# An eight-stage transformer megakernel on one core: first attention with 16-bit integer exponentials and column-grouped value matmuls, fourth with scores computed twice and weights loaded during the norm

## The chip, the cores and the metric

One Trainium2 chip, one of its cores. The metric is the device time of one execution in microseconds (us). The engines are TensorE (PE, with its weight loads shown apart as PEld), VectorE (DVE), ScalarE (ACT), GpSimd (POOL), SyncE (SP) and the DMA queues.

## The reference, cut to what matters

The activations `x` are 8 batches of 128 tokens of width 256. Four layers follow one another, each a cross attention and a feed-forward block, all residual:

```
x = x + L0_xattn(layernorm(x), ctx)      x = x + L0_ffn(layernorm(x))
x = x + L1_xattn(layernorm(x), ctx)      x = x + L1_ffn(layernorm(x))
x = x + L2_xattn(layernorm(x), ctx)      x = x + L2_ffn(layernorm(x))
x = x + L3_xattn(layernorm(x), ctx)      x = x + L3_ffn(layernorm(x))
```

The change touches two of the eight stages. In L0_xattn, 16 heads of 16 columns attend over all 1024 context tokens, and q, k, v and the probabilities are fake-quantized:

```
def _fq_sym(x, axis):      # scale = max|x| / 127, round, clip
def _fq_unsigned(x, axis): # scale = max(x) / 255, round, clip to 0..255
```

So the largest exponential of a row is 255 steps and every probability is a whole number of steps. In L3_xattn, 16 query heads share 4 key and value heads (4 groups of 4 heads, 16 columns each); each batch attends to its own 128 context tokens, with a linear position bias and a mask:

```
Q = (query @ Wq) / 4;  K = key @ Wk;  V = value @ Wv
scores = Q K^T + slope[head] * (k_pos - q_pos)
scores = where(mask, scores, lowest)
out = softmax(scores) @ V;  return out @ Wo
```

## The kernel before, in words

`program` runs a table of stages, `l0x`, `l0f`, `l1x`, `l1f`, `l2x`, `l2f`, `l3x`, `l3f`. Each is a `norm` block (layer norm and transpose to `x_normT`) and then the block or blocks of the stage itself; within a block each engine has its own instruction list, held together by semaphores. A stage may give `norm` a `Preload`, whose DMAs are issued on SP during the norm.

**First attention (`attention_l0`).** A first block (tiles `l0p_`) makes the quantized operands: `qT` and `kT` with 48 rows, `v` in bf16. The second block (tiles `l0m_`) is a software pipeline over N = 128 steps, one step for one batch b and head h, written out. Per step n:

- PE `score(n)` (L1747): two bf16 matmuls of 512 columns into one of three PSUM tiles `s_ps[n % 3]`; it waits until the exponential of step n-3 has left that tile.
- DVE `top(n)` (L1814): maximum over 1024 columns.
- POOL (L1737): the bias, log 255 minus scale times maximum.
- ACT `exps(n)` (L1794): exponential of 1024 columns to `pf` (f32), with the row sum.
- DVE `rounding(n-2)` (L1820): adds and subtracts a large constant, writing whole numbers in bf16 to `pi`, 4 buffers.
- SP: one DMA transpose `pi` to `pT`, 4 buffers.
- PE `value(n-5)` (L1757): eight matmuls, each with a 128x128 tile of `pT` as weights and 16 columns of `v` moving; the result has tokens on the partitions.

DVE's order in a step is top(n), then rounding(n-2). After a batch of 16 steps come `scale` on DVE (L1824, L1827), `turn_output` on PE (L1766), `keep_output` on ACT (L1800), `output` on PE (L1772) and `add` on DVE (L1832), at fixed steps:

```
SCALE, TURN, KEEP, OUT, ADD = H + LAG, H + LAG + 1, H + LAG + 1, H + LAG + 2, H + LAG + 3
```

with H = 16 and LAG = 5.

**Second attention (`attention_l1`)**, untouched: it computes each score tile twice, once to take the maximum (L824) and once transposed with the maximum folded in as an extra row (L844), so that ACT can write the transposed probabilities straight away. It works on 32-row and 32-column tiles of the array (L824, L844: 32 rows; L860: 32 columns, four column tiles in turn).

**Fourth attention (`attention_l3`).** SP loads four weights and the mask at the start of its own block (L981, L982). POOL makes 16 slope tiles (L991). PE computes V for all batches (L998). Then each batch has a projection of q and k (L1007) and four groups g of four heads; per group: PE `score` (L1013, 512 columns), DVE adds the slope (L1128), applies the mask limit (L1130) and takes the maximum (L1133), ACT makes four exponentials of 128 columns with sums (L1087), PE transposes them (L1019), DVE copies them to SBUF (L1138), PE multiplies with V (L1028). Per batch follow scaling (L1142, L1145), two transposes (L1036), a copy (L1093), the output projection (L1042) and the add (L1151). `carried` (L706) runs the batches in a loop of two.

Of the kernel before, what the change touches and what calls it, by code (L numbers as in the profile page):

```python
# [8 lines left out]
I16 = mybir.dt.int16  # L9
# [929 lines left out]
def attention_l3(pg):  # L939

    nc, G, J, C = pg.nc, 4, 4, 16
    FMAX = float(np.finfo(np.float32).max)
    names = ("w_in", "mask_in", "mask_step", "limits", "rel", "slopes", "proj", "proj_kept", "v_done", "v_kept", "scores", "biased", "steps", "maxed",
             "exped", "p_turned", "p_kept", "pv", "scaled", "o_turned", "o_kept", "out", "added", "recips")
    s = {m: pg.sem(f"l3x_{m}") for m in names}
    with ExitStack() as st:
# [17 lines left out]
        p = sb("p", [P, G, J, P])
        pT = sb("pT", [P, 2, J, P])
        mx = sb("mx", [P, 2, J])
        sm = sb("sm", [P, 2, G, J])
        rs = sb("rs", [P, 2, G, J])
        on = sb("on", [P, 2, D])
        oT = sb("oT", [P, 2, KD, P])  # L970
        pr = [psum(f"pr{i}", [P, G, P]) for i in range(2)]
        s_ps = [psum(f"s{i}", [P, J, P]) for i in range(2)]
        t_ps = [psum(f"t{i}", [P, J, P]) for i in range(2)]
        o_ps = psum("o", [P, 512])
        f_ps = psum("f", [P, 512])
        block = st.enter_context(nc.Block())

        @block.sync
        def _(sp):
            for m, t in (("l3_wq", wq), ("l3_wk", wk), ("l3_wv", wv), ("l3_wo", wo)):  # L980
                sp.dma_start(t[:], pg.dram[m]).then_inc(s["w_in"], 16)  # L981
            sp.dma_start(mask[:], pg.dram["mask"].rearrange("b t -> (b t)").unsqueeze(0).to_broadcast([P, T])).then_inc(s["mask_in"], 16)  # L982

        @block.gpsimd
        def _(pool):
            nc.gpsimd.iota(rel[:], [[1, P]], 0, -1, allow_small_or_imprecise_dtypes=True).then_inc(s["rel"], 1)
            nc.gpsimd.memset(kT[:], 0.0).then_inc(s["rel"], 1)
# [1291 lines left out]
```

## Time and profile before

| | |
|---|---|
| device time, 3 runs | 2201.01, 2208.95, 2210.03 us (median 2208.95) |
| profiled execution | 2183.78 us, span 2181.7 us |
| mean granted TensorE clock | 0.838 |
| busy share PE / DVE / ACT / POOL | 78% / 58% / 40% / 35% |
| instructions | 27158 |
| block `l0m_` of the first attention | 86.5 to 352.3 us |
| block of the fourth attention | 1748.4 to 1922.5 us |

The busy time is a sum over eight stages with different limits, so the two blocks are read by themselves: the span's start is zero, and a stretch is named by its two times. A granted clock of 1.00 is TensorE at 2.4 GHz, 0.50 at 1.2 GHz.

### The profile page before, as it was taken

To read this page: it belongs to the slowest core of one execution; us is meant where nothing else is said; L and a number is where in the kernel's file an instruction comes from. 1 tells how busy PE (TensorE), PEld (TensorE's weight loads), DVE (VectorE), ACT (ScalarE), POOL (GpSimd) and SP (SyncE) were. 2 spreads that over 40 slices of the span, in tenths; PEclk is the share of its full clock that TensorE was granted. 3 is DMA by queue.
4 is the path that set the end of the run, shared out by engine and by line. 5 is a ranking of instruction groups with operands and counts; after the bars stand their busy time and mean duration, and the time that the engine had idled before them with its cause. 6 is when DMAs were issued, how large, how long until landed. Compare 5 with 4: busy or idle time off the path is not lost. (4 is left out here: it accounts for less than half of the span.)

```text
span 2181.7 us, 27158 instructions
## 1 busy us (share of the span) xinstructions
PE 1693.7 (78%) x8684; PEld 1067.4 (49%) x8684; DVE 1259.9 (58%) x2770; ACT 870.7 (40%) x2109; POOL 761.6 (35%) x1440
## 2 busy tenths in 40 slices
PE   6677775999687499994488888888599878845773
PEld 5322223565454255553266666666355566634551
DVE  4889885222654633326688888888522336674335
ACT  2766663111322111113377777777311135421221
POOL 0133231000100298301588888887000020005773
PEclk8755555999787699997799999999799978867897
DMA  1266563111402022111100000000111000044655
GB/s 65 47 138 126 128 134 79 41 36 36 155 1 99 33 68 102 55 52 44 34 1 1 1 1 1 1 1 1 32 36 36 22 28 0 0 173 135 222 182 223
DMA packets 174473, 140.37 MB, mean 64 GB/s; under 512 B 142049, under 2 KB 154849, under 8 KB 170642
## 3 DMA queue, kind: packets, MB, share of 16 engines
q1 hardware_dynamic: 165026, 113.84, 18.2%
q0 software_dynamic: 7104, 23.60, 3.3%
q10 hardware_dynamic: 2224, 1.47, 0.2%
q8 instruction: 59, 0.97, 0.2%
q14 instruction: 60, 0.49, 0.1%
HBM read 85.82 MB, written 19.50 MB: 48 GB/s over the span
## 5 line engine op out<-in xcount | busy, mean ns | idle before, releaser
L1794 ACT ACTIVATE l0m_pf<-l0m_s,l0m_bias,l0x_sq 128x1024 f32<-128x1024 f32 x128 | 154.2, 1204 | 86.9 <-POOL l0m_bias L1737 86.7
L1814 DVE TENSOR_REDUCE l0m_mx<-l0m_s 128x1 f32<-128x1024 f32 x128 | 155.4, 1216 | 35.3 <-PE l0m_s L1747 35.2
L1368 PE MATMUL l2x_pr<-l_w,l2x_xq 128*128 128x512 bf16 x576 | 142.1, 384 | 40.5 <-ACT credits L42 40.5
L1737 POOL TENSOR_SCALAR l0m_bias<-l0m_mx,l0x_nsq 128x1 f32<-128x1 f32 x128 | 79.1, 618 | 261.3 <-DVE l0m_mx L1814 261.3
L318 PE MATMUL l1e_gu<-x_normT,l1e_w 128*128 128x512 f32 x384 | 169.5, 594 | 0.3 <-DVE l1e_h L361 0.3
L1497 DVE TENSOR_SCALAR l2x_raw<-l2x_raw,l2x_mv,l2x_rs 128x128 f32<-128x128 f32 x384 | 128.8, 396 | 21.5 <-POOL l2x_rs L1347 21.1
L1747 PE MATMUL l0m_s<-l0x_kT,l0x_qT 48*128 48x512 bf16 x256 | 131.6, 618 | 12.0 <-PEq L1572 4.1
L359 DVE TENSOR_TENSOR l1e_h<-l1e_sil,l1e_gu 128x512 f32<-128x512 f32 x48 | 33.0, 687 | 165.4 <-ACT l1e_sil L344 157.8
L318 PE MATMUL l0e_gu<-x_normT,l0e_w 128*128 128x512 f32 x272 | 120.1, 595 | 0.0
L318 PEld LDWEIGHTS l1e_gu<-x_normT,l1e_w 128*128 128x128 f32 x384 | 73.3, 191 | 83.4 <-issue 81.0
L1757 PEld LDWEIGHTS l0m_o<-l0x_v,l0m_pT 128*128 128x128 bf16 x1024 | 37.4, 106 | 156.5 <-DMA l0m_pT<-l0m_pi 113.8
L318 PE MATMUL l2e_gu<-x_normT,l2e_w 128*128 128x512 f32 x256 | 113.7, 598 | 0.0
L344 ACT ACTIVATE l1e_sil<-l1e_gu 128x512 f32<-128x512 f32 x48 | 28.7, 597 | 211.0 <-PE l1e_gu L318 211.0
L1347 POOL TENSOR_TENSOR l2x_rs<-l2x_rs,l2x_half 128x4 f32<-128x4 f32 x96 | 107.0, 1115 | 7.5
L1487 DVE BATCH_NORM_STATS2 l2x_bn<-l2x_raw 128x6 f32<-128x128 f32 x384 | 83.2, 278 | 40.7 <-ACT l2x_raw L1436 40.7
L1368 PEld LDWEIGHTS l2x_pr<-l_w,l2x_xq 128*128 128x128 bf16 x576 | 56.9, 99 | 96.5 <-ACT credits L42 40.9
L359 DVE TENSOR_TENSOR l0e_h<-l0e_sil,l0e_gu 128x512 f32<-128x512 f32 x34 | 23.4, 687 | 125.2 <-ACT l0e_sil L344 125.2
L1441 ACT ACTIVATE x_norm<-l2x_s,l2x_mx 128x128 f32<-128x128 f32 x256 | 90.2, 371 | 2.1 <-DVE l2x_mx L1492 2.1
L359 DVE TENSOR_TENSOR l2e_h<-l2e_sil,l2e_gu 128x512 f32<-128x512 f32 x32 | 22.0, 687 | 118.4 <-ACT l2e_sil L344 118.4
L1820 DVE TENSOR_SCALAR l0m_pi<-l0m_pf 128x1024 bf16<-128x1024 f32 x128 | 87.1, 681 | 1.5 <-ACT l0m_pf L1794 1.5
L326 PE MATMUL l1e_y<-l1e_w,l1e_h 128*128 128x256 f32 x384 | 86.6, 379 | 0.0
L1757 PE MATMUL l0m_o<-l0x_v,l0m_pT 128*128 128x16 bf16 x1024 | 48.8, 177 | 48.1 <-DMA l0m_pT<-l0m_pi 36.3
(507 smaller groups left out, 4076.8 us busy)
## 6 DMA issues: line engine op xcount, KB each, us to landing
l3m_w<-in_l_moe SPq DMA_DIRECT2D x16, 1280.0 KB, 6.7
l1e_w<-in_l_ffn SPq DMA_DIRECT2D x24, 384.0 KB, 3.0
l_rows<-zero_row SPq DMA_DIRECT2D x8, 1024.0 KB, 11.1
l_w<-l_rows SPq DMA_DIRECT2D x8, 1024.0 KB, 11.8
l0e_w<-in_l_ffn SPq DMA_DIRECT2D x17, 384.0 KB, 3.0
l2e_w<-in_l_ffn SPq DMA_DIRECT2D x16, 384.0 KB, 3.0
l1e_route<-l_route SPq DMA_DIRECT2D x8, 512.0 KB
l2q_wps<-in_l_wp SPq DMA_DIRECT2D x16, 256.0 KB, 2.7
```

What stands on the lines that cost most here:

```text
L318: last = nc.tensor.matmul(gu[half][:, m, :], w[:, slot, (2 * k + m) * P:(2 * k + m + 1) * P], pg.xnT[:, k, half * HALF:(half + 1) * HALF], ...
L326: last = nc.tensor.matmul(y[:, t, :], h[:, slot, t * P:(t + 1) * P], w[:, slot, WG:CHUNK], start=False, stop=False, skip_group_check=True)
L1347: g.tensor_tensor(rs[:, buf, 1, :], var, half[:, 0], ALU.pow).then_inc(s["rstd"], 1)
L1368: last = nc.tensor.matmul(flat(pr[t % 2][:]), src[:, k, tokens], pg.l2_w3[:, part, k, at:at + W], start=(k == 0 and part == 0), stop=(k == ...
L1441: last = nc.scalar.activation(p[:, a % 2, j, :], s_ps[a % 2][:, j, :], ACT.Exp, bias=mx[:, a % 2, j:j + 1], accum_out=sm[:, a % 2, j:j + 1])
L1487: last = nc.vector.bn_stats(bn[:, (2 * pi[1] + t) % 4, j, :], raw[:, (2 * pi[1] + t) % 4, j, :])
L1497: last = nc.vector.tensor_scalar(raw[:, buf, j, :], raw[:, buf, j, :], mv[:, buf, j, 0:1], rs[:, buf, 1, j:j + 1], ALU.subtract, ALU.mult)
L1747: last = nc.tensor.matmul(s_ps[n % 3][:, g * HALF:(g + 1) * HALF], qT[:, h, b * P:(b + 1) * P], kT[:, h, g * HALF:(g + 1) * HALF], start=T ...
L1757: last = nc.tensor.matmul(o_ps[:, h * C:(h + 1) * C], pT[:, n % 4, k, :], v[:, k, h * C:(h + 1) * C], start=(k == 0), stop=(k == B - 1))
L1794: nc.scalar.activation(pf[:, n % 4, :], s_ps[n % 3][:], ACT.Exp, scale=sq[:, b, h:h + 1], bias=bias[:, n % 4:n % 4 + 1], accum_out=sm[:, b ...
L1814: nc.vector.tensor_reduce(mx[:, n % 4:n % 4 + 1], s_ps[n % 3][:], AX, ALU.max).then_inc(s["maxed"], 1)
L1820: nc.vector.tensor_scalar(pi[:, n % 4, :], pf[:, n % 4, :], ROUND, ROUND, ALU.add, ALU.subtract).then_inc(s["rounded"], 1)
```

## The change

In the first attention: `pf` becomes int16, so the exponential is rounded as ACT writes it, and the rounding becomes a cast from int16 to bf16. `pi` and `pT` have 8 buffers. `v` is laid out with 32 columns per head, the upper 16 zero (a POOL memset in the first block), and is now the weight operand, `pT` the moving one with 128 columns; four heads write to four groups of 32 PSUM partitions. The result has tokens on the columns, so ACT copies it to SBUF (`read_output`), PE turns it back with four transposes (`turn_back`), and DVE scales from there. The steps after a batch lie further apart.

In the fourth attention: weights are a `Preload` during the norm. Projections of all batches run first, 512 columns at a time, and DVE writes `qT` and `kT` with extra rows that carry position, mask and maximum. Scores are computed twice as in the second attention, on 32-row tiles, through a ring of two PSUM tiles; maxima go through a transpose (`turn_max`) and one add (`augment`). V carries a column of ones, so the sums come out of the value matmul. POOL has one iota and 18 memsets. The mask comes over ACT's queue. The batches are written out.

```diff
-            pf = sb("pf", [P, 4, T])
-            pi = sb("pi", [P, 4, T], BF16)
-            pT = sb("pT", [P, 4, B, P], BF16)
+            pf = sb("pf", [P, 4, T], I16)
+            pi = sb("pi", [P, 8, T], BF16)
+            pT = sb("pT", [P, 8, B, P], BF16)
-            SCALE, TURN, KEEP, OUT, ADD = H + LAG, H + LAG + 1, H + LAG + 1, H + LAG + 2, H + LAG + 3
-            STEPS = N + LAG + 4
+            READ, BACK, SCALE, TURN, KEEP, OUT, ADD = (H + LAG + i for i in (0, 3, 4, 7, 7, 10, 11))
+            STEPS = N + LAG + 12
...
+        N, GROUP, LAG = B * H, 4, 6
...
+                def value(m):
+                    b, g = divmod(m, H // GROUP)
+                    for j in range(GROUP):
+                        n = GROUP * m + j
+                        pe.wait_ge(moved[n % 8], 16 * (n // 8) + 16)
+                    if g == 0 and b >= 1:
+                        pe.wait_ge(s["o_read"], b)
                     for k in range(B):
+                        for j in range(GROUP):
+                            last = nc.tensor.matmul(o_ps[32 * j:32 * j + 32, g * P:(g + 1) * P], v[:, k, GROUP * g + j, :],
+                                                    pT[:, (GROUP * m + j) % 8, k, :], start=(k == 0), stop=(k == B - 1))
                     last.then_inc(s["pv"], 1)
+                def turn_back(b):
+                    pe.wait_ge(s["o_read"], b + 1)
+                    if b >= 1:
+                        pe.wait_ge(s["added"], b)
+                    for g in range(H // GROUP):
+                        last = nc.tensor.transpose(f_ps[:, g * P:(g + 1) * P], oS[:, b % 2, g * P:(g + 1) * P], pg.ident[:])
+                    last.then_inc(s["o_back"], 1)
...
+                def read_output(b):
+                    act.wait_ge(s["pv"], (b + 1) * H // GROUP)
+                    nc.scalar.activation(oS[:, b % 2, :], o_ps[:], ACT.Copy).then_inc(s["o_read"], 1)
...
-                    nc.vector.tensor_scalar(pi[:, n % 4, :], pf[:, n % 4, :], ROUND, ROUND, ALU.add, ALU.subtract).then_inc(s["rounded"], 1)
+                    nc.vector.tensor_copy(pi[:, n % 8, :], pf[:, n % 4, :]).then_inc(s["rounded"], 1)
```

```diff
+def l3_preload(pg, stack):
+    return Preload(pg, stack, "l3w", [("wv", [P, KD, 64], d["l3_wv"]), ("wq", [P, KD, 4 * P], d["l3_wq"]), ("wk", [P, KD, P], d["l3_wk"]),
+                                      ("wo", [P, KD, D], d["l3_wo"])])
...
+        ring = [psum(f"r{i}", [P, 2, J * P]) for i in range(2)]
...
+            for i in range(B + 3):
+                if i < B:
+                    score(i, 0)
+                if 0 <= i - 1 < B:
+                    turn_max(i - 1)
+                if i < B:
+                    score(i, 1)
+                if 0 <= i - 2 < B:
+                    value(i - 2)
+                if 0 <= i - 3 < B:
+                    turn_output(i - 3)
+                if 0 <= i - 1 < B:
+                    shift(i - 1, 0)
+                    shift(i - 1, 1)
+                if 0 <= i - 2 < B:
+                    turn_back(i - 2)
+                if 0 <= i - 3 < B:
+                    output(i - 3)
```

Two places on PE show how the order moves. The first is the end of a batch in the first attention; `l0m_s` are scores, `l0m_o` values, `l0m_f` the output path. Before:

```order
L1747 MATMUL l0m_s<-l0x_kT,l0x_qT 128x512 x2
L1757 MATMUL l0m_o<-l0x_v,l0m_pT 128x16 x8
L1766 MATMUL l0m_f<-ident,l0m_on 128x128 x2
L1747 MATMUL l0m_s<-l0x_kT,l0x_qT 128x512 x2
L1757 MATMUL l0m_o<-l0x_v,l0m_pT 128x16 x8
L1772 MATMUL l0m_f<-l0w_wo,l0m_oT 128x256 x2
L1747 MATMUL l0m_s<-l0x_kT,l0x_qT 128x512 x2
```

and with the change:

```order
L1819 MATMUL l0m_s<-l0x_kT,l0x_qT 128x512 x8
L1832 MATMUL l0m_o<-l0m_pT,l0x_v 32x128 x32
L1841 MATMUL l0m_f<-ident,l0m_oS 128x128 x4
L1819 MATMUL l0m_s<-l0x_kT,l0x_qT 128x512 x8
L1832 MATMUL l0m_o<-l0m_pT,l0x_v 32x128 x32
L1847 MATMUL l0m_f<-ident,l0m_on 128x128 x2
L1819 MATMUL l0m_s<-l0x_kT,l0x_qT 128x512 x6
L1853 MATMUL l0m_f<-l0w_wo,l0m_oT 128x256 x2
L1819 MATMUL l0m_s<-l0x_kT,l0x_qT 128x512 x2
```

The value matmuls of four steps stand together after the fourth score, four transposes are new, and the output projection stands three steps behind its transposes instead of one.

The second place is one batch of the fourth attention (`l3x_r` is the ring, `l3x_po` the values). With the change:

```order
L1050 MATMUL l3x_r<-l3x_kT,l3x_qT 128x128 x8
L1058 MATMUL l3x_nmT<-ident,l3x_nm 128x128 x4
L1050 MATMUL l3x_r<-l3x_kT,l3x_qT 128x128 x8
L1074 MATMUL l3x_po<-l3x_pT,l3x_v 32x512 x4
L1090 MATMUL l3x_f<-ident,l3x_on 128x128 x2
L1066 MATMUL l3x_r<-l3x_qa,l3x_kT 128x512 x4
L1082 MATMUL l3x_bk<-ident,l3x_oS 128x128 x4
L1096 MATMUL l3x_f<-l3w_wo,l3x_oT 128x256 x2
```

Before, the last quarter of a batch's work in the loop read:

```order
L1013 MATMUL l3x_s<-l3x_kT,l3x_qT 128x512
L1019 MATMUL l3x_t<-ident,l3x_p 128x128 x4
L1036 MATMUL l3x_f<-ident,l3x_on 128x128 x2
L1023 REGISTER_ALU
L1028 ISA
L1028 MATMUL l3x_o<-l3x_v,l3x_pT 128x16 x4
L1042 MATMUL l3x_f<-l3x_wo,l3x_oT 128x256 x2
```

The score, transposes and values that came four times per batch are replaced by one longer list per batch, and the projections (16 matmuls per batch before) now stand ahead of the first score.

## Rows read from the trace of the kernel before

**Rows 1.** Busy time by stretch; the columns stand in the first line.

```profile
core 0: us, PE busy (x) PEld busy (x) DVE busy (x) ACT busy (x) POOL busy (x), PEclk, DMA share, GB/s
86.50:352.30 265.80, 194.53 (x1328) 65.18 (x1328) 230.46 (x280) 170.71 (x273) 79.05 (x128) 0.50 0.62 127
99.00:122.00 23.00, 18.63 (x132) 5.41 (x130) 23.00 (x27) 17.31 (x27) 8.31 (x13) 0.50 0.71 151
615.70:621.50 5.80, 5.80 (x66) 3.66 (x58) 2.69 (x3) 1.94 (x2) 0.00 (x0) 0.84 0.01 3
1748.40:1922.50 174.10, 143.18 (x784) 113.40 (x784) 94.41 (x159) 79.47 (x307) 12.88 (x18) 0.81 0.03 9
```

**Rows 2.** Groups by line, 86.5 to 352.3 us: busy, mean ns | idle before, releaser.

```profile
L1814 DVE TENSOR_REDUCE l0m_mx<-l0m_s 128x1 f32<-128x1024 f32 x128 | 155.4, 1216 | 35.3 <-PE l0m_s L1747 35.2
...
L1820 DVE TENSOR_SCALAR l0m_pi<-l0m_pf 128x1024 bf16<-128x1024 f32 x128 | 87.1, 681 | 1.5 <-ACT l0m_pf L1794 1.5
```

**Rows 3.** Timeline of one ordinary step, first attention: start us, us, instruction.

```profile
103.22 0.68 DVE L1820 TENSOR_SCALAR l0m_pi<-l0m_pf 128x1024 bf16<-128x1024 f32 x1
...
103.24 0.38 PE L1757 MATMUL l0m_o<-l0x_v,l0m_pT 128*128 128x16 bf16 x8 [0.26 <-DMA l0m_pT<-l0m_pi]
103.40 0.64 POOL L1737 TENSOR_SCALAR l0m_bias<-l0m_mx,l0x_nsq 128x1 f32<-128x1 f32 x1 [1.09 <-DVE l0m_mx L1814]
...
103.69 1.03 PE L1747 MATMUL l0m_s<-l0x_kT,l0x_qT 48*128 48x512 bf16 x2
103.82 1.21 DVE L1814 TENSOR_REDUCE l0m_mx<-l0m_s 128x1 f32<-128x1024 f32 x1
104.07 1.21 ACT L1794 ACTIVATE l0m_pf<-l0m_s,l0m_bias,l0x_sq 128x1024 f32<-128x1024 f32 x1 [0.44 <-POOL l0m_bias L1737]
...
104.96 0.68 DVE L1820 TENSOR_SCALAR l0m_pi<-l0m_pf 128x1024 bf16<-128x1024 f32 x1
```

**Rows 4.** Timeline behind the first batch of the first attention.

```profile
129.08 2.08 PE L1772 MATMUL l0m_f<-l0w_wo,l0m_oT 128*128 128x256 f32 x4 [1.91 <-ACT l0m_oT L1800]
...
131.09 1.03 PE L1747 MATMUL l0m_s<-l0x_kT,l0x_qT 48*128 48x512 bf16 x2
...
132.06 0.38 PE L1757 MATMUL l0m_o<-l0x_v,l0m_pT 128*128 128x16 bf16 x8
132.16 1.22 DVE L1814 TENSOR_REDUCE l0m_mx<-l0m_s 128x1 f32<-128x1024 f32 x1 [3.38 <-PE l0m_s L1747]
...
132.37 1.03 PE L1747 MATMUL l0m_s<-l0x_kT,l0x_qT 48*128 48x512 bf16 x2
...
133.48 0.27 POOL L1737 TENSOR_SCALAR l0m_bias<-l0m_mx,l0x_nsq 128x1 f32<-128x1 f32 x1 [4.57 <-DVE l0m_mx L1814]
```

**Rows 5.** Groups by line and shape: DVE, 1024 elements of two bytes.

```profile
L1172 DVE TENSOR_SCALAR l2q_step<-l2q_z 128x1024 int16<-128x1024 int16 x8 | 4.0, 500 | 0.3
...
L1173 DVE TENSOR_SCALAR l2q_step<-l2q_step 128x1024 bf16<-128x1024 bf16 x8 | 3.4, 427 | 0.3
```

**Rows 6.** Timeline of the second attention: values (L860), scores (L824), shifted scores (L844).

```profile
620.14 0.61 PE L860 MATMUL l1x_po<-l1x_pT,l1x_ones 128*32 128x256 f32 x8
...
620.57 0.61 PE L860 MATMUL l1x_po<-l1x_pT,l1x_vz 128*32 128x256 f32 x8
...
621.55 1.16 PE L844 MATMUL l1x_r<-l1x_qa,l1x_cb 32*128 32x256 f32 x16
...
623.84 0.73 PEld L824 LDWEIGHTS l1x_r<-l1x_cb,l1x_qm 32*128 32x128 f32 x8 [0.17 <-ACT l1x_pT L890]
...
628.08 1.15 PE L860 MATMUL l1x_po<-l1x_pT,l1x_vz 128*32 128x256 f32 x8
...
628.93 1.15 PE L860 MATMUL l1x_po<-l1x_pT,l1x_ones 128*32 128x256 f32 x8
```

**Rows 7.** Groups by line, page: f32 matmuls of 512 columns in a dense stage.

```profile
L318 PE MATMUL l1e_gu<-x_normT,l1e_w 128*128 128x512 f32 x384 | 169.5, 594 | 0.3 <-DVE l1e_h L361 0.3
```

**Rows 8.** Timeline of the fourth attention: its V matmuls, then its last batches.

```profile
1754.22 7.09 PE L998 MATMUL l3x_s<-l3x_wv,ctxT 128*128 128x64 f32 x32 [6.53 <-DMA l3x_wo<-in_l_wo]
...
1912.96 0.44 PE L1036 MATMUL l3x_f<-ident,l3x_on 128*128 128x128 f32 x2 [0.82 <-DVE l3x_on L1145]
...
1914.05 1.11 PE L1042 MATMUL l3x_f<-l3x_wo,l3x_oT 128*128 128x256 f32 x4
...
1914.99 0.60 PE L1019 MATMUL l3x_t<-ident,l3x_p 128*128 128x128 f32 x4
...
1922.10 0.42 DVE L1151 TENSOR_TENSOR x_res<-x_res,l3x_f 128x256 f32<-128x256 f32 x1 [2.38 <-PE l3x_f L1042]
```

**Rows 9.** Groups by line, 1748.4 to 1922.5 us: DVE waiting for scores.

```profile
L1128 DVE TENSOR_TENSOR l3x_sc<-l3x_s,l3x_slope 128x512 f32<-128x512 f32 x32 | 22.0, 687 | 50.5 <-PE l3x_s L1013 50.4
```

More of the change, by code:

```diff
@@ new lines, in attention_l3 @@
+        nmT, po, bk, f = (psum(m, [P, J * P]) for m in ("nmT", "po", "bk", "f"))
+        banks = [ring[0][:, 0], ring[0][:, 1], ring[1][:, 0], ring[1][:, 1], nmT[:], po[:], bk[:], f[:]]
+        block = st.enter_context(nc.Block())
+        jobs = [("q", 0, j) for j in range(J)] + [("k", 0, 0), ("k", 1, 0)] + [("q", 1, j) for j in range(J)]
+        kept_after = []
+        for what, half, j in jobs:
+            kept_after.append((kept_after[-1] if kept_after else 0) + (4 if what == "k" else 1))
@@ L1032, in turn_output @@
-            def turn_output(b, u):
-                pe.wait_ge(s["scaled"], b + 2)
-                pe.wait_ge(s["added"], b + 1)
+            for n, (what, half, j) in enumerate(jobs):
+                if n == 7:
+                    pe.wait_ge(s["v_kept"], 1)
+                elif n >= 8:
+                    pe.wait_ge(s["proj_kept"], kept_after[n - 8])
+                w, src = (wq[:, :, tile(j)], pg.xnT) if what == "q" else (wk[:], pg.ctxT)
+                for k in range(KD):
+                    last = nc.tensor.matmul(banks[n % 8], w[:, k, :], src[:, k, half * HALF:(half + 1) * HALF], start=(k == 0), stop=(k == KD - 1))
+                last.then_inc(s["proj"], 1)
@@ new lines, in score, with turn_max @@
+            def score(b, pr):
+                ps = freed(pe, "s", b, pr)
+                if b == 0 and pr == 0:
+                    pe.wait_ge(s["proj_kept"], kept_after[-1])
+                for j in range(J):
+                    for jj in range(2):
+                        g = 2 * pr + jj
+                        last = nc.tensor.matmul(ps[:, jj, tile(j)], qT[rows(g), j, tile(b)], kT[rows(g), tile(b)], start=True, stop=True)
+                last.then_inc(s["scores"], 1)
+            def turn_max(b):
+                pe.wait_ge(s["maxed"], 2 * b + 2)
+                if b >= 1:
+                    pe.wait_ge(s["augmented"], b)
+                for j in range(J):
+                    last = nc.tensor.transpose(nmT[:, tile(j)], nm[:, b % 2, j, :], pg.ident[:])
+                last.then_inc(s["nm_turned"], 1)
```

383 lines of the change are left out of this document (195 added, 188 removed).

## The prediction

> **What bounds the kernel now.** I read the stretches first. The two blocks that change are 265.8 and 174.1 us of the profiled 2183.78 [rows 1]; nothing else is touched, so the whole answer lies in these two.
>
> In the first attention DVE is busy for 23.00 of 23.00 us in an ordinary stretch, and the granted clock is 0.50 (1.2 GHz) throughout [rows 1]. The timeline says why a step takes what it takes: from one rounding to the maximum behind it 0.60 us, from there to the next rounding 1.14 us, together 1.74 us [rows 3]. Durations overlap a little, so the start-to-start times count, not 1.21 + 0.68. ACT waits 0.44 us in each step for POOL's bias [rows 3], so it isn't the bound. But 128 x 1.74 = 222.7 us is 43.1 us less than the block takes. Most of the rest stands behind each batch: PE waits 1.91 us for ACT's copy, then projects for 2.0 us, all ahead of the next score, and DVE sits idle for 3.38 us [rows 4]. Over the 128 maxima DVE waits 35.2 us for scores [rows 2]. Seven such places are about 24 us. The other 19 us are fill, drain and DVE's small operations.
>
> In the fourth attention PE is busy for 143 of 174 us and DVE waits 50.4 us for scores [rows 1, 9]: PE and the chain through it are the bound. 6.5 us at its start are a wait for the last weight [rows 8].
>
> **First attention, part by part.** *The cast.* The rounding reads f32 and takes 681 ns [rows 2]; the cast reads and writes two bytes. No row has an int16 to bf16 cast. The nearest are 427 ns (bf16 to bf16) and 500 ns (an integer operation) on 1024 elements [rows 5]; the outer bound is no gain, 681. I take 427, since the arithmetic is float, which puts the interval at 0.60 - 0.25 = 0.35 us and DVE's step at 1.49. The Trainium skill (Vector Engine (DVE) Microarchitecture Reference, 5.1) lets a cast run at four elements per cycle when source and target both have two-byte types, int16 not excepted; by it the value would be 427 as well. POOL's bias takes 0.64 us when it starts during a rounding and 0.27 when it does not [rows 3, 4]; a shorter cast lets it go sooner, so the chain gets no longer.
>
> *The bubble behind a batch.* The projection now stands three steps behind its transposes, and ACT's copy is done by then. The 24 us go. In their place comes PE work.
>
> *PE's load at 1.2 GHz.* Two scores and one value step repeat every 1.28 us when PE runs unhindered (131.09 to 132.37): 0.96 for the scores, 0.32 for eight value pairs, so 40 ns a pair [rows 4]. A value group is now 32 pairs with 128 moving columns on four column tiles. The same shape in f32 with 256 columns costs 54 ns a matmul at 2.4 GHz (8 from 620.14 to 620.57) and 106 ns at 1.2 GHz (628.08 to 628.93) [rows 6]. That is twice the columns and f32; four tiles plainly run side by side there. A bf16 pair here has a quarter of that array work, 27 ns, so something else sets its pace. Bounds: 27 and 106 ns. I take 40, the pace at which pairs went before. A group is then 1.3 us, plus 0.3 for switching in and out (0.17 us stand ahead of a change of tile shape in the second attention, [rows 6]). Per batch: 16 x 0.96 = 15.4, four groups 6.4, four new transposes 1.3 (twice the 0.60 of rows 8, at half the clock), two more 0.7, projection 2.0: 25.8 us. DVE needs 16 x 1.49 + 1.0 = 24.8. So PE is 1.0 us a batch above DVE, 8 us in all.
>
> *The burst.* Score n+1 stands behind a whole group now. The ring has three tiles; with a step of 1.49 us a score has some 0.3 us of slack, and it comes about 1.0 us late. At worst that leaves DVE 0.7 us idle in each of 32 groups, 22 us; at best nothing, if PE catches up in the steps between. I take half, 11 us. ACT's extra copy of 512 columns (half of the 1.21 us for 1024, so 0.6 a batch) fits into the 0.44 us a step that ACT waits.
>
> *DMA.* Transposes use 0.71 of the engines at 1.74 us a step [rows 1], 1.23 us each, so a step of 1.5 us fits; eight buffers and a lag of six steps cover their latency.
>
> *Ends.* The last batch gets a copy and four transposes more, 2.5 us. POOL's memset of `v` lies in a block where POOL is idle and costs nothing.
>
> Sum: 128 x 1.49 = 190.7, plus 19 + 2.5 + 8 + 11 = 231 us against 265.8: **34 us less** (bounds: 54 less with neither PE term; about 10 less with the full burst and a pair at 50 to 60 ns).
>
> **Fourth attention.** The weights arrive during the norm, and the 6.5 us go. V is 32 instructions in 7.1 us, as before. Projections: 10 jobs of 2 f32 matmuls, 40 instructions of 512 columns at 169.5/384 = 0.44 us [rows 7], 17.6 us, and some 3.5 more because V runs at 1.2 GHz. DVE's setup (four additions over 1024 columns and small ones, some 8 us) lies beside V, its copies beside the projections. With the last copy the first score starts 29 us into the block.
>
> Per batch on PE at 2.4 GHz: scores 32 instructions at 91 ns (eight loads in 0.73, [rows 6]) 2.9; shifted scores 8 instructions, two row tiles side by side at 0.44/2, 1.8 (L844's 16 in 1.16 go faster, on shorter columns); values 8 x 0.11 = 0.9; transposes 0.6 + 0.6 + 0.44, projection 1.1 [rows 8]; six changes of tile shape at 0.25, 1.5. Together 9.8 us. DVE needs two maxima of 1.22, an add of 0.69, scaling and adding 1.1: 4.2; ACT two exponentials of 1.21 and two copies of 0.6 and 0.4: 3.4. Both are hidden as long as the ring of two tiles does not lock. I add 7% for stretches at 1.2 GHz (the second attention's clock was 0.84 with PE busy all the time, [rows 1]): 10.5 x 8 = 84. Fill and drain across three batches' lag: 8. Block: 29 + 84 + 8 = 121 against 174.1: **53 us less** (bounds: 65 at 2.4 GHz throughout and faster shifts, 38 with 12.4 us a batch).
>
> **The time.** 34 + 53 = 87 less than the profiled 2183.8 is 2096.8. That execution is 25 us under the median of the three runs, so for a median I take 2208.95 - 87 = 2122. I call no change what lies within 0.5%.
>
> **Rivals.**
>
> *A, PE's clock rises in the first attention.* It stays at 0.50 with PE busy 18.63 of 23.00 us, while a stretch with PE busy throughout had 0.84 [rows 1]. The changed loop keeps PE busy some 93% at 1.2 GHz, between the two. If it is granted 2.4 GHz for most of the loop, both PE terms (8 + 11) vanish: 106 less, 2103. Against it: at 2.4 GHz the same work fills half the time, and the clock may fall again.
>
> *B, the value pairs cost more than 40 ns.* The Trainium skill (TensorEngine Tiling (Array Packing), Feature Incompatibilities) says that column tiling excludes the fast weight load. By the page on TensorE: Matmul & The Clock Gate (LDWEIGHTS) 32 columns then take 27 ns, as an estimate; if they do not overlap the matmuls, a group grows by 0.9 us and the sum would be 2150. From rows: halfway between 40 and 106 ns, some 70, a group is 1.0 us longer, 31 us in all, and 56 less remains: 2153. For it: nothing shows this shape in bf16. Against it: 54 ns for the larger f32 form.
>
> *C, the ring of two locks the fourth attention.* A tile goes score, maximum, shifted score, exponential, and PE reaches each in list order. If PE's other 4.5 us a batch fall inside that chain, a batch takes some 14 us, the block loses 28 us of its gain, 59 less in all: 2150. Against it: the second attention, with three tiles, kept PE busy 5.80 of 5.80 us.
>
> *D, slower: the 32-wide tiles do not run side by side.* Then a pair costs 107 ns at 1.2 GHz, a group 3.7 us, a batch 34 us and the first attention 295 (+29); in the fourth scores cost 6.3, shifts 3.4, values 3.4, a batch 17.4 and the block about 176 (+2): 2240. It decides when pairs stay above 100 ns in both. The L860 rows speak plainly against it.
>
> **Chances.** Forecast 0.54, A 0.22, B 0.13, C 0.07, D 0.04. Forecast, A, B and C are all faster by over 0.5%, and only their joint failure lands near zero: faster 0.93, same 0.03, slower 0.04. The range must take in A with its bound and B and C with some spread of the runs (the three span 9 us): 2088 to 2168.
>
> **What would show it.** Right: the cast at about 430 ns, DVE busy over 90% of an ordinary stretch, no 3.4 us idle behind a batch, 32 value matmuls in 1.3 us, and a fourth-attention block of about 121 us with the first score 29 us in. Wrong: a cast at 681 ns or more; DVE waiting for scores after each value group by more than 0.7 us; value groups over 2 us; in the fourth attention, PE waiting for exponentials.

## The result and the profile after

The changed kernel takes **2077.5 us** in the median of four runs (2074.3 to 2080.6), the kernel before 2206.8 beside it (2201.0 to 2210.0). The ratio is 0.9417, 95% interval 0.9388 to 0.9445: 129 us less, where 87 were forecast. The time lies 10.5 us under the range.

The two blocks and the last stage by stretch, changed kernel (columns as in [rows 1]):

```profile
84.80:308.50 223.70, 181.91 (x1360) 62.94 (x1360) 198.65 (x280) 174.14 (x281) 46.75 (x128) 0.52 0.78 151
99.00:122.00 23.00, 18.34 (x140) 4.57 (x132) 22.27 (x31) 19.51 (x31) 5.57 (x15) 0.50 0.90 171
1705.40:1791.30 85.90, 80.51 (x569) 46.73 (x568) 48.93 (x80) 24.82 (x35) 2.85 (x19) 0.94 0.01 3
1793.10:2072.50 279.40, 154.62 (x672) 118.86 (x672) 118.80 (x321) 54.30 (x143) 126.81 (x133) 0.71 0.52 183
```

The first attention went from 265.8 to 223.7 us, 42 less, and the fourth from 174.1 to 85.9, 88 less [rows 1]. That is 130, as the medians say. The profiled executions alone (2183.8 and 2074.3) differ by 109 only, because the last stage, which no edit touches, took 257.3 us in the one and 279.4 in the other. The first experiments ask whether the change has a part in that.

The first attention, groups by line (changed kernel, 84.8 to 308.5 us), against [rows 2]:

```profile
L1903 DVE TENSOR_REDUCE l0m_mx<-l0m_s 128x1 f32<-128x1024 f32 x128 | 156.0, 1220 | 21.8 <-PE l0m_s L1819 20.5
L1909 DVE CAST l0m_pi<-l0m_pf 128x1024 bf16<-128x1024 int16 x128 | 53.5, 418 | 0.7 <-ACT l0m_pf L1877 0.7
L1916 DVE TENSOR_TENSOR l0m_on<-l0m_f,l0m_rs 128x256 f32<-128x256 f32 x8 | 3.4, 425 | 7.4 <-PE l0m_f L1841 6.7
L1921 DVE TENSOR_TENSOR x_res<-x_res,l0m_f 128x256 f32<-128x256 f32 x8 | 3.3, 413 | 3.6 <-PE l0m_f L1853 3.6
```

The cast takes 418 ns, the rounding took 681. One group of values and the steps beside it, timeline of the changed kernel, against [rows 3]:

```profile
103.27 1.22 DVE L1903 TENSOR_REDUCE l0m_mx<-l0m_s 128x1 f32<-128x1024 f32 x1
...
104.36 1.04 PE L1832 MATMUL l0m_o<-l0m_pT,l0x_v 128*32 128x128 bf16 x32
104.40 0.42 DVE L1909 CAST l0m_pi<-l0m_pf 128x1024 bf16<-128x1024 int16 x1
104.58 0.37 POOL L1809 TENSOR_SCALAR l0m_bias<-l0m_mx,l0x_nsq 128x1 f32<-128x1 f32 x1 [1.10 <-DVE l0m_mx L1903]
...
104.74 1.22 DVE L1903 TENSOR_REDUCE l0m_mx<-l0m_s 128x1 f32<-128x1024 f32 x1
104.99 1.20 ACT L1877 ACTIVATE l0m_pf<-l0m_s,l0m_bias,l0x_sq 128x1024 int16<-128x1024 f32 x1 [0.17 <-POOL l0m_bias L1809]
...
105.34 2.02 PE L1819 MATMUL l0m_s<-l0x_kT,l0x_qT 48*128 48x512 bf16 x4
...
129.98 0.78 PEld L1832 LDWEIGHTS l0m_o<-l0m_pT,l0x_v 128*32 128x32 bf16 x32 [0.84 <-issue]
129.98 1.05 PE L1832 MATMUL l0m_o<-l0m_pT,l0x_v 128*32 128x128 bf16 x32
```

DVE's step is 1.47 us (103.27 to 104.74). The 32 value matmuls go from 104.36 to the next score at 105.34: 0.98 us, 31 ns a pair at 1.2 GHz, switching included. A pair is one weight load and its matmul; the last two lines show the loads and the matmuls of a later group.

The fourth attention, one batch on PE from the timeline of the changed kernel, with DVE's two maxima:

```profile
1756.94 1.21 PE L1066 MATMUL l3x_r<-l3x_qa,l3x_kT 32*128 32x512 f32 x8
...
1758.09 0.66 PE L1082 MATMUL l3x_bk<-ident,l3x_oS 128*128 128x128 f32 x4
...
1758.58 1.03 PE L1096 MATMUL l3x_f<-l3w_wo,l3x_oT 128*128 128x256 f32 x4
...
1759.54 1.16 PE L1050 MATMUL l3x_r<-l3x_kT,l3x_qT 32*128 32x128 f32 x16
...
1760.63 0.66 PE L1058 MATMUL l3x_nmT<-ident,l3x_nm 128*128 128x128 f32 x4
1760.75 1.23 DVE L1196 TENSOR_REDUCE l3x_nm<-l3x_r 128x8 f32<-128x1024 f32 x1 [0.68 <-PE l3x_r L1050]
...
1761.22 1.16 PE L1050 MATMUL l3x_r<-l3x_kT,l3x_qT 32*128 32x128 f32 x16
...
1762.31 1.07 PE L1074 MATMUL l3x_po<-l3x_pT,l3x_v 128*32 128x512 f32 x8
1762.49 1.22 DVE L1196 TENSOR_REDUCE l3x_nm<-l3x_r 128x8 f32<-128x1024 f32 x1
...
1763.30 0.44 PE L1090 MATMUL l3x_f<-ident,l3x_on 128*128 128x128 f32 x2
...
1763.67 1.21 PE L1066 MATMUL l3x_r<-l3x_qa,l3x_kT 32*128 32x512 f32 x8
```

Start to start: scores 1.09 (twice), maxima turned 0.59, values 0.99, output turned 0.37; and in the batch ahead, shifted scores 1.15 (1756.94 to 1758.09), outputs turned back 0.49, projection 0.96 (1758.58 to 1759.54). Together 6.73 us, and the first score of one batch to that of the next (1752.81 to 1759.54) is 6.73 us as well. PE is busy 37.94 of the 40 us from 1750 to 1790, which take in the drain of the last batches, at a granted clock of 1.00. The forecast had 10.5 us a batch. In the kernel before, the additions of neighbouring batches lay 14.5 to 20.0 us apart, the last pair left out. No run takes the new loop apart against the old one: of the 88 us, only the preload is priced by itself (below), and what the tiles, the twofold scores and the early projections each give is not shown.

### The profile page after: what moved, and what is told of

Its sections match the earlier page's. It is cut to its first block and busy times, and to the rows that moved or that the text cites. A ratio compares the mean times of both kernels' runs of the same rounds, so it can differ in the third digit from the quotient of the medians.

```text
span 2072.5 us, 26189 instructions
## 1 busy us (share of the span) xinstructions
PE 1625.8 (78%) x8459; PEld 1007.3 (49%) x8500; DVE 1184.5 (57%) x2689; ACT 818.3 (39%) x1844; POOL 725.8 (35%) x1442
## 5 line engine op out<-in xcount | busy, mean ns | idle before, releaser
L1877 ACT ACTIVATE l0m_pf<-l0m_s,l0m_bias,l0x_sq 128x1024 int16<-128x1024 f32 x128 | 154.1, 1204 | 39.1 <-POOL l0m_bias L1809 39.1
L1434 PE MATMUL l2x_pr<-l_w,l2x_xq 128*128 128x512 bf16 x538 | 133.9, 384 | 42.9 <-ACT credits L42 40.9
L1819 PE MATMUL l0m_s<-l0x_kT,l0x_qT 48*128 48x512 bf16 x256 | 123.5, 609 | 38.4 <-ACT l0m_pf L1877 33.7
L1809 POOL TENSOR_SCALAR l0m_bias<-l0m_mx,l0x_nsq 128x1 f32<-128x1 f32 x128 | 46.8, 365 | 222.3 <-DVE l0m_mx L1903 220.9
L2023 POOL DMA_INDIRECT l3m_xg<-l_xw,l3m_idx x64 | 61.9, 967 | 62.1 <-DVE l3m_idx L2182 41.3
L326 PEld LDWEIGHTS l1e_y<-l1e_w,l1e_h 128*128 128x128 f32 x384 | 73.0, 190 | 19.7 <-issue 10.5
L2028 POOL DMA_INDIRECT l_rows<-ctx_tok,l3m_slot x64 | 63.8, 997 | 51.3 <-ACT ctx_tok L2132 34.1
## 6 DMA issues: line engine op xcount, KB each, us to landing
l2q_wps<-in_l_wp SPq DMA_DIRECT2D x16, 256.0 KB, 2.7
```

Source lines behind the costliest of these rows:

```text
L326: last = nc.tensor.matmul(y[:, t, :], h[:, slot, t * P:(t + 1) * P], w[:, slot, WG:CHUNK], start=False, stop=False, skip_group_check=True)
L1434: last = nc.tensor.matmul(flat(pr[t % 2][:]), src[:, k, tokens], pg.l2_w3[:, part, k, at:at + W], start=(k == 0 and part == 0), stop=(k == ...
L1819: last = nc.tensor.matmul(s_ps[n % 3][:, g * HALF:(g + 1) * HALF], qT[:, h, b * P:(b + 1) * P], kT[:, h, g * HALF:(g + 1) * HALF], start=T ...
L1877: nc.scalar.activation(pf[:, n % 4, :], s_ps[n % 3][:], ACT.Exp, scale=sq[:, b, h:h + 1], bias=bias[:, n % 4:n % 4 + 1], accum_out=sm[:, b ...
L2028: g.indirect_dma_start(out=rows, out_offset=bass.IndirectOffsetOnAxis(ap=slot[:, e:e + 1], axis=0), in_=ye[:, e % NY, :], in_offset=None). ...
```

## The experiments

All runs in one table. *Maxima* is from the first to the last maximum of the first attention, *fourth* from the first statistics of the fourth layer's norm before its attention to those of the norm behind it, *last* from there to the end; all from DVE's rows. The *fourth* column also holds a difference of the clock that no edit made: V's matmuls ran at either of two clocks, which moves the stretch by up to 7 us (see *The weights*).

| run | ratio to before (95%) | maxima | fourth | last |
|---|---|---|---|---|
| before, profiled | 1 | 252.4 | 184.2 | 257.3 |
| changed, first result | 0.9417 (0.9388 to 0.9445) | 208.2 | 95.0 | 279.4 |
| x1 first attention alone | 0.9795 (0.9774 to 0.9817) | 208.0 | 179.9 | 257.9 |
| x2 fourth alone | 0.9628 (0.9606 to 0.9650) | 250.6 | 101.9 | 260.8 |
| x3 projection spaced | 0.9922 (0.9891 to 0.9953) | 235.2 | 180.7 | 262.3 |
| x4 own weights | 0.9471 (0.9448 to 0.9494) | 207.7 | 109.2 | 257.6 |
| x5 changed, again | 0.9413 (0.9380 to 0.9445) | 207.7 | 101.9 | 256.0 |
| x6 float rounding | 0.9497 (0.9463 to 0.9531) | 228.0 | 99.6 | 256.5 |
| x7 cast alone | 0.9891 (0.9859 to 0.9923) | 228.7 | 180.9 | 262.1 |
| x8 column tiles in turn | 0.9537 (0.9506 to 0.9567) | 238.4 | 99.7 | 255.8 |
| x9 ends apart | 0.9445 (0.9422 to 0.9468) | 211.1 | 101.9 | 278.4 |
| x10 half projection | 0.9418 (0.9395 to 0.9442) | 208.3 | 97.6 | 280.9 |
| x12 shifts apart | 0.9483 (0.9459 to 0.9506) | 208.2 | 109.8 | 279.3 |
| x13 scores together | 0.9438 (0.9414 to 0.9462) | 208.0 | 101.7 | 279.6 |
| x14 apart and spaced | 0.9416 (0.9388 to 0.9444) | 206.1 | 102.0 | 255.6 |
| x15 changed, third time | 0.9405 (0.9378 to 0.9431) | 207.7 | 95.0 | 256.2 |
| x16 row tiles in turn | 0.9505 (0.9477 to 0.9532) | 207.9 | 117.4 | 261.7 |

**Do the blocks add up?** Each attention changed alone (the other function as before).

> The kernel before with the new first attention alone. Theory S (the two blocks gain what their own stretches show, 42 and 88 us, and the last stage simply takes another time from one execution to the next): about 42 us under before in the median (2165), the first block some 224 us, the fourth 174; the last stage anywhere from 257 to 279 us. Theory T (the changed kernel makes the last stage 22 us longer, 279 against 257, through what the fourth attention leaves behind it): the last stage is back at 257 here. By my prediction's sum the block would give 34.

> The kernel before with the new fourth attention alone. Theory S: about 88 us under before (2119), the fourth block 86 us, and the sum of this gain and that of the first attention alone is the whole, 129. Theory T: the last stage takes 279 us here and the gain is nearer 66. By my prediction's sum the block would give 53.

> The changed kernel once more, beside the variants of it. Theory S: its last stage (from the fourth layer's norm before the experts to the end) takes as long as that of the other kernels on the same chip, some 258 to 262 us and not 279, and its time is under 2060 us if before is at 2184, with the same ratio of 0.94. Theory T: the last stage stays at 279 us.

Before took 2183.7 us beside the first two and 2187.0 beside the third; the three took 2139.0, 2104.0 and 2058.5. The gains are 2.05% and 3.72% (45 and 80 us), together 5.8%, as the whole. The second is 8 us short of the 88 expected: in x2, as in x5, V ran at 1.2 GHz and the fourth stretch took 101.9 us, not 95. The last stage of the changed kernel is 256.0 us in x5:

```profile
1699.70:1801.60 101.90, 91.20 (x584) 54.80 (x584) 55.78 (x108) 29.69 (x46) 2.85 (x19) 0.83 0.04 12
1801.60:2057.60 256.00, 139.04 (x672) 106.34 (x672) 117.75 (x321) 55.12 (x143) 126.43 (x133) 0.77 0.56 199
```

Theory S holds and T falls. Where before, measured beside the others, took 2184 to 2187 us, the last stage of every kernel profiled took 256 to 262 us; where it took 2204 and 2207 us, 278 to 281. The changed kernel itself stands on both sides (279.4, then 256.0 and 256.2), so it goes with which runs were measured together and not with the kernel; x9 to x13 (278 to 281) ran on another chip than the other experiments. Before has no profile among the long ones.

**What the order of the first attention is worth.** x3 is before with `OUT, ADD = H + LAG + 4, H + LAG + 5` for `+ 2, + 3`:

> Before, with the projection of a batch two steps later (and the addition with it), nothing else. Theory: the 3.4 us bubble behind a batch is PE waiting for ACT's copy; then seven bubbles shrink to well under 1 us and the block gets 15 to 24 us shorter, the step staying at 1.74. Rival: DVE's bubble comes from the projection itself and the switch into it, which is only moved; then under 7 us.

0.8% less (17 us by the ratio, 15 by the medians), and the maxima span 17 us less. Of the seven 5.2 us steps behind a batch six became 2.7 us and one 3.3; the step stayed at 1.74. DVE's waits for scores (84 to 345 us; waiter, releaser, total, times, longest) fell from 35.2 us [rows 2] to 18.0:

```profile
DVE l0m_mx L1814 <- PE l0m_s L1747: 18.0, 12, 9.5
```

The longest, 9.5 us, stands ahead of the first maximum in every one of these kernels, so behind it 25.7 us became 8.5. The bubble was the wait for ACT's copy. What remains in each of those steps is DVE waiting some 0.9 us for a score that stands behind the projection's 2 us on PE.

**What the cast is worth.** x6 puts the rounding back into the changed kernel, x7 puts the cast alone into the kernel before:

```
-  pf = sb("pf", [P, 4, T], I16)
+  pf = sb("pf", [P, 4, T])
-  nc.vector.tensor_copy(pi[:, n % 8, :], pf[:, n % 4, :])
+  nc.vector.tensor_scalar(pi[:, n % 8, :], pf[:, n % 4, :], ROUND, ROUND, ALU.add, ALU.subtract)
```

> The changed kernel with f32 exponentials and the old rounding; grouped values, spacing and buffers stay. The cast theory: DVE's step goes back from 1.47 to 1.74 us, 127 steps, so 34 us longer, and POOL's bias is back at 0.64 us; what stands behind a batch shrinks by 1 to 5 us in all, since a longer step gives PE slack. Rival (the step is set by the chain through POOL and ACT, not by DVE): less than 20 us.

> Before with 16-bit exponentials and the cast, nothing else. If the parts add: the step goes from 1.74 to 1.47 us, 34 us less, and the bubble of 3.5 us behind a batch stays. Rival: the loop needs the later changes to use it (four buffers of transposed exponentials, transposes of 1.3 us each and PE's eight value pairs a step on top of two scores): the step stays above 1.55 and under 24 us are gained.

The step moved as expected, 1.74 against 1.47, in both. The time did not: the cast brings 20.3 us of maxima with the new order (228.0 to 207.7) and 23.7 without (252.4 to 228.7), not 34. Most of the rest comes back as DVE waiting for PE. Waits of DVE for the scores, x6 and then x5 (as above):

```profile
DVE l0m_mx L1903 <- PE l0m_s L1819: 11.4, 7, 9.5
```

```profile
DVE l0m_mx L1903 <- PE l0m_s L1819: 20.1, 22, 9.5
```

With 1.74 us steps PE keeps up but for the first 9.5 us; with 1.47 it does not. The waits account for 8.7 of the 14 us that came back between x6 and x5; where the others lie is not shown. In time x6 costs 17 us (2075.7 against 2058.5), as its rival said, but not for the rival's reason: the step is DVE's, and 10 (x7) to 14 us (x6) of the 34 that it gives come back. The fourth stretch, where V ran faster in x6, hides 2.3 us of the 20.3.

**Do the column tiles work at once?** x8 issues a value group's loops as `for j ... for k` instead of `for k ... for j`, so eight matmuls in a row stand on one tile.

> The changed kernel with the 32 value matmuls of a group issued tile by tile instead of going round the four column tiles. Side-by-side theory: eight in a row on one tile cannot overlap, a pair costs some 107 ns instead of 30, a group 3.4 us instead of 1.0; PE then needs 16 x 0.96 + 4 x 3.4 + 4 = 33 us a batch against DVE's 24.8, and the first attention gets 50 to 65 us longer. Rival (weights, not tiles, set the pace): same time within 5 us.

```profile
105.21 2.25 PE L1832 MATMUL l0m_o<-l0m_pT,l0x_v 128*32 128x128 bf16 x32
...
105.59 1.21 DVE L1903 TENSOR_REDUCE l0m_mx<-l0m_s 128x1 f32<-128x1024 f32 x1
...
108.47 1.23 DVE L1903 TENSOR_REDUCE l0m_mx<-l0m_s 128x1 f32<-128x1024 f32 x1 [1.33 <-PE l0m_s L1819]
```

A group takes 2.2 us instead of 1.0, at the same granted clock of 0.50; each costs DVE 1.4 us, and the maxima span 30.7 us more (27 in the median). So going round the tiles is worth 1.2 us a group, but not the factor I expected: 69 ns a pair in turn, not 107. The 50 to 65 us expected became 31. That a pair on one tile costs no more than 69 ns, while 128 columns of a score matmul take 120 at the same clock (0.96 us for two of 512 columns), suggests that something overlaps there too; what it is, no run shows. Later in the loop the granted clock was a little higher than in the changed kernel (0.58 and 0.55 against 0.52), which makes the 31 us a lower bound for the order alone.

**The ends of a batch.** x9 sets BACK, SCALE, TURN, KEEP to +4, +5, +8, +8 (one step later, away from the value groups), x14 also OUT, ADD to +12, +13:

> The changed kernel with the four transposes back and the two transposes of a batch's output each one step later, so that neither stands in the same step as a value group. Theory: PE's pieces of 1.0 us and 1.1 us in one step are what makes DVE wait for the scores behind a batch (3.2 us beyond the steps per batch, 1.1 of it DVE's own work), apart they fit into the slack: 0.8 to 1.2 us less a batch, 6 to 9 us in all. Rival (PE is short of time over the whole batch, so the wait only moves): within 2 us.

> As the run with the ends one step later, but the output projection now stands four steps behind its transposes instead of two, so that ACT's copy is done. Theory: the 3.73 us step of that run is the old bubble come back (PE waited 0.95 us for the copy, then 2.0 us of projection ahead of the next score); with it gone, what stands behind a batch falls from 3.2 to about 2 us, 5 to 9 us less than the changed kernel. Rival (PE has no slack over the batch, so each move only shifts the wait): within 2 us.

Both missed. In x9 the projection stood two steps behind its transposes, and the bubble was back:

```profile
134.33 2.08 PE L1853 MATMUL l0m_f<-l0w_wo,l0m_oT 128*128 128x256 f32 x4 [0.95 <-ACT l0m_oT L1887]
...
137.41 1.23 DVE L1903 TENSOR_REDUCE l0m_mx<-l0m_s 128x1 f32<-128x1024 f32 x1 [2.17 <-PE l0m_s L1819]
```

x14 mended that and the maxima span 1.6 us less than the changed kernel's, its time is the same. Its waits sit behind the projection, whose four f32 matmuls take 2.0 us at 1.2 GHz wherever they stand. The rival is right: what is left is PE's work, moved about.

**What sets a batch of the fourth attention.**

> The changed kernel, the fourth attention's output projection reduced to the first of its two halves of the inner dimension (half of the sum is left out): 2 of 4 instructions, 0.48 us a batch. PE theory (a batch is the sum of PE's pieces, 6.73 us): a batch falls to 6.25 us, 4 us in all. Ring theory (the chain score, maximum, shifted score, exponential through two tiles sets the batch, and PE's pieces lie inside it): a batch stays above 6.6 us.

> The changed kernel, with the transposes back put between the two pairs of shifted scores of a batch, so that at most two of the four row tiles can work at once. My prediction took two tiles at once, 1.8 us for both pairs; the trace shows 1.14. Four-tile theory: apart each pair takes 0.9 us at 2.4 GHz, 0.6 to 0.9 us more a batch, 5 to 7 us in all. Rival (512 columns in f32 go faster than I took them, whatever stands beside them): within 2 us.

> The changed kernel, with both halves of a batch's scores issued as one piece that goes round all four row tiles. If four tiles work at once, 32 instructions take 1.1 us instead of 2.2; PE then needs 5.6 us a batch. PE theory: the batch follows, 6.7 to 5.7 us, 8 us in all. Ring theory: both tiles of the ring must be free before a score, so two maxima (2.4 us) and two exponentials (2.0 us) end one after the other outside the scores; 1.1 + 2.5 + 0.6 + 2.0 = 6.2 us a batch, 2 to 5 us in all, or none.

> The changed kernel, with the fourth attention's scores issued row tile by row tile (eight instructions in a row on one tile) instead of alternating between two. 16 instructions took 1.09 us on two tiles and 32 took 1.10 us on four, so the pace goes with the number of tiles: one tile should give 2.2 us for 16, 2.2 us more a batch, some 17 us in all. My prediction's 91 ns an instruction, were it a fixed price, would give no change within 2 us.

*x10*, timeline:

```profile
1758.25 0.60 PE L1096 MATMUL l3x_f<-l3w_wo,l3x_oT 128*128 128x256 f32 x2
1758.87 1.16 PE L1050 MATMUL l3x_r<-l3x_kT,l3x_qT 32*128 32x128 f32 x16
```

A batch is 6.39 us (maxima at 1760.07 and 1766.46). The piece itself went from 0.96 to 0.62 us, and the batch followed by exactly that: PE's sum sets it. Half of the instructions took off 0.34 us and not the 0.48 expected, so some 0.3 us of a piece do not go with their number.

*x12*, timeline:

```profile
1765.77 1.13 PE L1066 MATMUL l3x_r<-l3x_qa,l3x_kT 32*128 32x512 f32 x4
1766.83 0.66 PE L1082 MATMUL l3x_bk<-ident,l3x_oS 128*128 128x128 f32 x4
1767.42 1.13 PE L1066 MATMUL l3x_r<-l3x_qa,l3x_kT 32*128 32x512 f32 x4
1768.47 1.13 PE L1096 MATMUL l3x_f<-l3w_wo,l3x_oT 128*128 128x256 f32 x4
```

Each pair of shifted scores takes 1.06 us alone; both together had taken 1.15. Four row tiles had been at work at once, and the batch grows from 6.73 to 7.89 us (maxima at 1762.85 and 1770.74), the stretch to 109.8 us, 8 more than x13's beside it, where V ran at the same clock. That is more than the theory's 0.6 to 0.9 us a batch: the second pair costs 0.96, and the two changes of tile shape that the edit adds the other 0.2 (the transposes back take 0.59 us start to start where they had taken 0.49, the projection behind shifted scores 1.06 where it had taken 0.96). A change of shape costs about 0.1 us here.

*x13 and x16*, one batch's scores going round four tiles, and half of them on one tile at a time:

```profile
1756.02 1.17 PE L1059 MATMUL l3x_r<-l3x_kT,l3x_qT 32*128 32x128 f32 x32
1757.12 0.66 PE L1068 MATMUL l3x_nmT<-ident,l3x_nm 128*128 128x128 f32 x4
...
1758.96 1.22 DVE L1204 TENSOR_REDUCE l3x_nm<-l3x_r 128x8 f32<-128x1024 f32 x1
1759.19 2.17 PE L1076 MATMUL l3x_r<-l3x_qa,l3x_kT 32*128 32x512 f32 x8
...
1762.74 0.98 PEld L1059 LDWEIGHTS l3x_r<-l3x_kT,l3x_qT 32*128 32x128 f32 x32 [0.33 <-ACT l3x_pT L1137]
```

```profile
1769.13 1.71 PE L1050 MATMUL l3x_r<-l3x_kT,l3x_qT 32*128 32x128 f32 x16
1770.76 1.06 PE L1074 MATMUL l3x_po<-l3x_pT,l3x_v 128*32 128x512 f32 x8
```

An instruction of 128 columns costs 34 ns on four tiles (1.10 us for 32), 68 on two (1.09 for 16) and 102 on one (1.63 for 16), all at 2.4 GHz. Yet x13 gained nothing. PE saved 1.08 us on the scores and the shifted scores went from 1.15 to 2.10 (1759.19 to 1761.29), since the second pair now has to wait until DVE is through the second maximum, which ends at 1760.18. Scores, two maxima with an addition between them, the second pair, the second exponential, for which the next scores wait (1762.74): that chain is a batch of 6.73 us again. The ring theory is right there, though it had given 6.2. In x16 a batch takes 7.76 us, 1.0 more, where the theory had 2.2 (it had taken one tile for half as fast as two), and the fourth stretch grew by 15 to 22 us; the run is 1.0% slower than x15, 22 us, where I expected 17. Eight batches at 1.0 us more are only 8 of that. In two of the last four batches PE's values and shifted scores ran at 1.2 GHz, which they did not in the changed kernel, and such a batch took 9.33 us (columns as in [rows 1]):

```profile
1766.90:1774.66 7.76, 7.76 (x63) 5.20 (x62) 4.15 (x6) 2.83 (x5) 0.00 (x0) 1.00 0.00 0
1774.66:1783.99 9.33, 9.33 (x63) 5.53 (x62) 4.15 (x6) 2.90 (x5) 0.00 (x0) 0.82 0.01 2
```

So the total came near the forecast by luck: half the price on the tile, the rest from the clock.

**The weights.** x4 loads the four weights in the attention's own block (`pre.load` moved from the norm into a sync program there).

> The changed kernel, but the fourth attention's four weights are loaded in its own block instead of during the norm. Theory P (my prediction): 6.5 us longer, since only the wait comes back. Theory Q: while PE waits, the granted clock falls, V runs at 1.2 GHz as it did before (7.1 us instead of 3.8) and some projections too, so it is 10 to 13 us longer. Rival: under 3 us, since DVE's setup is what the first score waits for.

The wait is back, 8.3 us, and V runs at 1.2 GHz:

```profile
L1034 PE MATMUL l3x_f<-l3w_wv,ctxT 128*128 128x64 f32 x32 | 7.1, 423 | 8.3 <-DMA l3w_wo<-in_l_wo 8.3
```

But V's clock is no proof of theory Q. In the changed kernel itself it differs by execution, first the first result's, then x5's:

```profile
1706.21 3.76 PE L1030 MATMUL l3x_f<-l3w_wv,ctxT 128*128 128x64 f32 x32 [0.78 <-PEq L144]
```

```profile
1708.17 7.06 PE L1030 MATMUL l3x_f<-l3w_wv,ctxT 128*128 128x64 f32 x32 [0.78 <-PEq L144]
```

The fourth stretch is 95.0 us where V had 2.4 GHz (the first result and x15) and 101.9 in x5. V accounts for 3.3 of these 7 us; the projections right behind it (6.9 or 9.2 us for the first 16) and the first shifted scores for most of the others. The variants that leave this place as it is show the same: V took 7.06 us in x9, x12, x13, x14 and x16, and 4.6 to 4.7 in x6, x8 and x10. x4 has 109.2 us, so 7 or 14 more. The medians give 13 us (0.9471 against 0.9413 and 0.9405), with 9 us of interval on either side. Against x5, where V ran at the same clock, the preload is worth 7 us. Whether a late weight also makes the low clock likelier is not settled.

## Why the prediction was wrong

The sign, the two blocks, and most mechanisms were right: the cast at two-byte speed, 0.35 us from it to the next maximum, no 3.4 us idle behind a batch, DVE as the bound of the first attention and PE of the fourth. No rival happened: the clock of the first attention stayed at 0.52, and PE was busy 18.34 of 23.00 us of an ordinary stretch, not the 93% of the forecast (A), a pair took 31 ns (B), the fourth attention's batch is PE's sum (C), the tiles run side by side (D). What failed is size.

**First attention: 34 forecast, 42 measured.** By the prediction's own steps:

- *Cast.* Forecast 0.25 x 128 = 32 us, measured 0.27 x 127 = 34 off the steps (x6, x7). Right.
- *Bubble.* Forecast 24, measured 17 by spacing alone (x3) and 24.4 with all of the new order (252.4 to 228.0, x6); DVE's waits for scores behind the first maximum fell from 25.7 us to 8.5 and to 1.9. Right in size, but spacing, the forecast's only reason, gives 17 of it.
- *PE's load and burst.* Forecast 8 + 11 = 19 given back. From the two figures above, 34 + 24.4 - 44.4 (252.4 to 208.0) = 14 came back, and the old order without groups gave back 10 of the same 34 (x7). A batch on PE is 15.4 of scores, 4 x 0.98 = 3.9 of values, 1.05 + 0.62 of transposes and 2.0 of projection, 23 us, not 25.8: **a value group was taken at 1.6 us and is 0.98**. So PE stands 1.5 us a batch below DVE's 16 x 1.47 + 1.0 = 24.5, where the forecast had it 1.0 above. A group delays DVE by 0.2 us, not 0.35 (steps of 1.67 beside 1.47).
- *Ends.* Forecast 2.5 more; from the last maximum to the last addition it is 14.1 us against 11.9 before, 2.2 more. Right.

**Fourth attention: 53 forecast, 88 measured.** This is the step that failed, and with it the range:

- *Start.* The first score stands 29 us in by the forecast, 22.6 us in the first result and 28 in x5. At 1.2 GHz for V the forecast was good; at 2.4 GHz V took 3.8 us instead of 7.1, and the first projections 2.3 less. Up to 6.4 us, and that part is luck of the execution.
- *Per batch.* Forecast 9.8 us and 7% for the clock. Measured against it: scores 2.18 (2.9), shifted scores 1.15 (1.8), values 0.99 (0.9), transposes 1.45 (1.64), projection 0.96 (1.1), and no separate price for **six changes of tile shape (1.5)**: each piece starts where the one before it stops, and what a change costs, about 0.1 us by x12, lies in the start-to-start times. That is 3.1 us a batch, 25 in all. [Rows 6] had shown the shifted scores: 16 of 256 columns in 1.16 us is the array work of 8 of 512, and I set it aside as "on shorter columns" and took two tiles where x12 shows four. The scores I priced by the loads' 91 ns, x13 and x16 show the number of tiles to be what sets their pace.
- *Clock, fill and drain.* Forecast 5.6 + 8. First score to end is 63.2 us and eight batches are 53.8, so 9.4 for all three: 4 us less.

Changes of shape were charged on top in the first attention as well (0.3 of the 1.6 us). The evidence for them was misread: the 0.17 us ahead of 623.84 in [rows 6] are idle time of the weight loads, not of the matmuls, and the row puts them down to ACT. Both blocks missed on the same side: prices carried over from another shape were too high (40 ns a pair for 31; 91 and 220 ns an instruction of the fourth attention for 68 and 144), and a switch came on top of them.

*The baseline.* Counting from the median instead of from the profiled execution was right, and x1, x2 and x5 show why: the profiled execution of before has a last stage of 257 us, and where before takes 2204 us or more the kernels beside it had a last stage some 20 us longer. Its median of 2209 would belong to those; no profile of before shows it.

*The page.* The Trainium skill (TensorEngine Tiling (Array Packing), Feature Incompatibilities) says that column tiling excludes the fast weight load, and rival B made 0.9 us a group of it. The 32 weight loads of a group are busy for 0.78 us in all and lie under the matmuls, which take 0.98: nothing of such a price shows. The page may be right about the load, which no run compares; its price did not come on top of the matmuls.

## What to carry to other kernels

Price a piece of PE work by the start-to-start time of the nearest row with the same number of tiles at work and the same changes of shape around it, and add no switch to it. An f32 matmul of 128 columns on a 32-row tile cost 102, 68 and 34 ns with one, two and four tiles in turn, so order the loop to go round them; but see first whether the pieces can be ready together, or the gain comes back as a wait. When a step gets shorter on the bound engine, the next engine's bursts (a value group, a projection in f32 at 1.2 GHz) take back a part of it, here 10 to 14 of 34 us; spacing the chain copy, projection, addition by three steps removed the wait for the copy but not the projection's 2 us on PE. And compare blocks, not whole executions: an untouched stage differed by 22 us between two runs.

## What the runs showed of the hardware

- Instructions on row tiles, 128 columns f32 at 2.4 GHz: 102 ns each with one tile in turn, 68 with two, 34 with four. On column tiles, 128 columns bf16 at 1.2 GHz: 69 ns a pair in turn, 31 going round four.
- The V matmuls of the same kernel, behind the same PE work, ran at 2.4 GHz in two executions and at 1.2 GHz in one (3.76 and 7.06 us), and with the matmuls right behind them this made the fourth stretch 95 or 102 us. Why it differs stays open.
- A change of tile shape between pieces of PE work cost about 0.1 us at 2.4 GHz (x12).
- The last stage, full of gathers and scatters, takes 256 to 262 us or 278 to 281, alike for all kernels profiled together. The cause stays open.
